# A graph network with LSTM readout on one core: VectorE's preparation reordered, weights turned during the first layer, biases added in VectorE's evictions

## What is computed

```python
def L0(x, A):                              # graph layer with two batch norms
    A_norm = A + eye
    deg = sum(A_norm, 0) + sum(A_norm, 1) - diagonal(A_norm)
    A_hat = A_norm * rsqrt(deg)[:, None] * rsqrt(deg)[None, :]
    h = relu(batchnorm(einsum('nm,bmd->bnd', A_hat, x) @ W1.T + b1))   # 128 -> 256
    return batchnorm(h @ W2.T + b2)                                    # 256 -> 128

def L1(x, adj):
    h = relu(einsum('ts,bsh->bth', adj, x @ Wg0 + bg0))
    h = relu(einsum('ts,bsh->bth', adj, h @ Wg1 + bg1))
    for p in 1, 2, 3, 4:                   # LSTM over windows of p nodes
        last = lstm_last(Wih[p-1], Whh[p-1], bih[p-1], bhh[p-1], windows(h, p))
        h[:, p-1::p] = last
    return h

x = layernorm(x + L0(x, adj))
out = layernorm(x + L1(x, adj))
```

## Time and profile before

| what | value |
|---|---|
| time, median of 3 runs | 824.11 us (822.83 to 824.62) |
| the profiled execution: its own time, its span | 823.75 us, 821.8 us |
| TensorE busy, matmuls | 767.1 us (93%) |
| VectorE, ScalarE, GpSimd busy | 645.2, 565.2, 316.0 us |
| chain that ended last, by engine | PE 56%, DVE 11%, ACT 7% |
| first aggregate starts | 16.75 us |
| stage 2's first product starts | 117.19 us |
| second group's first product starts (group 1) | 202.89 us |
| stage 4's first product starts | 399.47 us |
| one group of stage 3, from the 3rd to the 14th | 13.31 us |

### The profile page before, as it was taken

How to read it: one execution, slowest core, us unless ns; L and a number is a source line. 1 busy time by engine, 2 the same in 40 slices (tenths; PEclk the granted TensorE clock), 3 DMA queues, 4 the chain that set the end, 5 groups by cost and what they waited for, 6 DMA issues and landing times.

```text
span 821.8 us, 11917 instructions
## 1 busy us (share of the span) xinstructions
PE 767.1 (93%) x3920; PEld 427.4 (52%) x3920; DVE 645.2 (79%) x1363; ACT 565.2 (69%) x892; POOL 316.0 (38%) x282
## 2 busy tenths in 40 slices
PE   3999969978999999999999999999999999999993
PEld 2666633336676767667544444444444444555441
DVE  5455557767677777775598878799999999998998
ACT  0777748854777777767788867777666757656662
POOL 0000000006886767764000000009087947376692
PEclk9999969997999999999999999999999999999997
DMA  6333130001313132320070000000100112102012
GB/s 173 102 100 102 51 102 0 0 0 50 104 53 104 51 104 65 91 76 28 0 307 1 1 1 0 1 1 1 39 26 15 39 39 84 67 18 65 1 39 90
DMA packets 63126, 45.06 MB, mean 55 GB/s; under 512 B 1593, under 2 KB 61538, under 8 KB 62050
## 3 DMA queue, kind: packets, MB, share of 16 engines
q1 hardware_dynamic: 63074, 44.40, 17.7%
HBM read 27.61 MB, written 16.78 MB: 54 GB/s over the span
## 4 chain that ended last, share of the span: by engine, by line
PE 56%; DVE 11%; ACT 7%; issue 1%; POOL 1%; DVEq 0%
PE ps L612 10%; PE ps L613 10%; PE ps L621 9%; PE ps L617 6%; PE ps L626 6%; PE ps L618 6%; ACT work L813 4%; PE ps L688 3%; DVE work L1002 3%; ACT work L820 2%; DVE store L1012 2%; DVE store L1007 2%; DVE work L988 1%; DVE store L1056 1%; PE ps L666 1%
## 5 line engine op out<-in xcount | busy, mean ns | idle before, releaser
L813 ACT ACTIVATE work<-ps,gate_bias 128x512 f32<-128x512 f32 (+1 forms) x449 | 279.7, 681 | 63.6 <-PE ps L626 45.7
L612 PE MATMUL ps<-store,wih 128*128 128x512 f16 (+1 forms) x449 | 168.9, 376 | 2.7 <-issue 1.5
L613 PE MATMUL ps<-store,wih 128*128 128x512 f16 (+1 forms) x449 | 168.9, 376 | 0.0
L621 PE MATMUL ps<-store,wih 128*128 128x512 f16 (+1 forms) x449 | 158.0, 376 | 0.0
L510 POOL TENSOR_TENSOR end_mv<-end_mv,minus_half 128x12 f32<-128x12 f32 (+1 forms) x16 | 30.8, 1926 | 266.1 <-DVE end_mv L1031 266.1
L1002 DVE TENSOR_TENSOR work<-work 128x512 f32<-128x512 f32 (+1 forms) x129 | 89.6, 695 | 36.9 <-ACT work L820 36.9
L501 POOL TENSOR_SCALAR ring<-ring,ln_mv 128x128 f32<-128x128 f32 x120 | 117.4, 991 | 2.7 <-POOL ln_mv L491 2.5
L820 ACT ACTIVATE work<-store 128x512 f32<-128x512 f32 (+1 forms) x97 | 60.5, 623 | 66.7 <-DVE store L995 51.9
L617 PE MATMUL ps<-store,whh 128*128 128x512 f16 (+1 forms) x248 | 93.1, 376 | 0.0
L618 PE MATMUL ps<-store,whh 128*128 128x512 f16 (+1 forms) x248 | 93.1, 376 | 0.0
L626 PE MATMUL ps<-store,whh 128*128 128x512 f16 (+1 forms) x248 | 93.0, 376 | 0.1
(11 more groups left out here) (124 smaller groups left out, 1229.3 us busy)
## 6 DMA issues: line engine op xcount, KB each, us to landing
ring<-in_x_dram SPq DMA_DIRECT2D x32, 256.0 KB, 2.9
ring<-in_x_dram SPq DMA_DIRECT2D x16, 512.0 KB, 5.2
x_scratch<-ring SPq DMA_DIRECT2D x16, 512.0 KB, 3.5
ring<-x_scratch SPq DMA_DIRECT2D x5, 1024.0 KB, 4.9
out_dram<-ring SPq DMA_DIRECT2D x5, 768.0 KB, 3.6
store<-x_scratch SPq DMA_DIRECT2D x3, 1024.0 KB, 14.1
out_dram<-store SPq DMA_DIRECT2D x3, 768.0 KB, 3.5
out_dram<-ring SPq DMA_DIRECT2D x5, 256.0 KB, 2.3
```

The lines of the kernel that those rows point to most:

```text
L612: nc.tensor.matmul(acc(j), w_hi, x_hi, start=True, stop=False)
L613: nc.tensor.matmul(acc(j), w_lo, x_hi, start=False, stop=False)
L621: last = nc.tensor.matmul(acc(j), weights(wih, j)[0], x_lo, start=False, stop=u.first)
L813: nc.scalar.activation(acts[:, n % 2, gate, 0:u.cols], ps[:, gate_bank(q), 0:u.cols], ACT.Tanh if gate == G else ACT.Sigmoid, bias=gate_bi ...
```

## The change

1. VectorE's preparation is put in another order. It starts when adj is loaded, without waiting for TensorE's transpose; `ahatT` becomes the 11th step, then w1T, `vec`, w2T, the row sums, four copies of `minus_c` = -(row sum x bg0) and the gate biases. Four steps (`u1_bias` = bg1 - minus_c by Wg1) come after chunk 8 of stage 1. The f16 splits are gone. Steps that nothing near needs no longer wait for themselves (`step` beside `link`). TensorE and ScalarE wait for the step they need instead of for the last.
2. TensorE turns the weights inside stage 1, one job behind the chunks 12, 14, ... 24, and so do ScalarE's and VectorE's parts of it. One 128-column product (for `u1_bias`) is added behind chunk 8. Stage 1's loops, and SyncE's loop of loads, are written out instead of being loops of the machine.
3. A small Sigmoid at ScalarE's start (`act_warm`) loads its function table; no other load of a table stands in ScalarE's list after it (before: one at the first copy, one at the first gate).
4. In stage 3 the bias products (L686, L706) are left out. With C = row sum x bg0, relu(z + C) = max(z, -C) + C: VectorE takes the maximum of the bank and `minus_c` (`relu_h0`), and adds `u1_bias` in the eviction of u1 (`bias_u1`), which brings in C by Wg1 and bg1. Both evictions move from ScalarE to VectorE. `hidden_hi` moves from VectorE to ScalarE for the units in the groups; in stage 4 it stays on VectorE. VectorE's and ScalarE's order within a group is new.
5. bg0 is loaded as one more small vector, ahead of the gate biases, and no longer broadcast.

The diff's core:

```diff
+            def turn_weights(job):
+                pe.wait_ge(ld_lstm, 32)
+                if job == 0:
+                    pe.wait_ge(prep_dve, PREP_STEPS)
                 wait(pe, w_lo_done, job - 1)
                 for j in range(4):
                     last = nc.tensor.transpose(ps[:, 6 + job % 2, j * P:(j + 1) * P],
                                                lstm_rows[:, job * 4 + j, :], ident[:])
                 last.then_inc(w_turned, 1)
 
+            pe.wait_ge(prep_dve, AHAT_STEP)
+            aggregate(0)
+            pe.wait_ge(ld_vec, 9 * 16)
+            nc.tensor.transpose(ps[:, 6, 0:P], vec_rows, ident[:]).then_inc(prep_pe, 1)
+            nc.tensor.matmul(ps[:, 5, 0:P], ones[:], adjT[:], start=True, stop=True).then_inc(prep_pe, 1)
+            pe.wait_ge(prep_dve, W1T_STEP)
+            for c in range(CHUNKS):
+                if c == 1:
+                    pe.wait_ge(prep_dve, RS_STEP)
+                if c + 1 < CHUNKS:
+                    aggregate(c + 1)
+                channels(c)
+                if c == U1_BIAS_AT:
+                    pe.wait_ge(prep_dve, MINUS_C_STEP)
+                    pe.wait_ge(ld_wg, 32)
+                    nc.tensor.matmul(ps[:, 6, 0:P], minus_c[:, 0, :], wg1_sb[:], start=True, stop=True)\
+                        .then_inc(prep_pe, 1)
+                if c in W_JOB_AT:
+                    turn_weights(W_JOB_AT.index(c))
 
...
-                    nc.tensor.matmul(ps[:, H0[h], :], bias_l[:, 0, :], bias_bt[:].rearrange("p b n -> p (b n)"),
-                                     start=True, stop=False)
                     nc.tensor.matmul(ps[:, H0[h], :], wg0_sb[:], z_slot(g)[:, h * CB:(h + 1) * CB, :].rearrange(
-                        "p b n -> p (b n)"), start=False, stop=True).then_inc(h0_summed, 1)
+                        "p b n -> p (b n)"), start=True, stop=True).then_inc(h0_summed, 1)
...
-                    nc.tensor.matmul(ps[:, GNN[h], :], bias_l[:, 1, :], bias_tb[:].rearrange("p n b -> p (n b)"),
-                                     start=True, stop=False)
                     by_time = ps[:, GNN[h], :].rearrange("p (n b) -> p n b", b=CB)
                     for b in range(CB):
                         last = nc.tensor.matmul(by_time[:, :, b], u1[:, h * CB + b, :], adjT[:],
-                                                start=False, stop=(b == CB - 1))
+                                                start=True, stop=True)
...
-            act.wait_ge(prep_dve, PREP_STEPS)
-
-            def copy_agg(c, q):
+            act.wait_ge(consts_done, 6)
+            nc.scalar.activation(act_warm[:], ones[:, 0:1], ACT.Sigmoid)
...
+            def hidden_hi(n):
+                u = UNITS[n]
+                act.wait_ge(hid_done, n + 1)
+                nc.scalar.activation(unit_output(u, 0), columns(acts[:, n % 2, O, :], u), ACT.Copy).then_inc(hi_done, 1)
...
-                relu_h0(g, 0)
-                relu_h0(g, 1)
                 for n in FILLS[g][:1]:
                     gates(n)
-                copy_u1(g, 0)
+                    tanh_cell(n)
+                for n in FILLS[g][1:]:
+                    gates(n, (0, 1))
                 for n in FILLS[g][:1]:
-                    tanh_cell(n)
-                copy_u1(g, 1)
+                    hidden_hi(n)
                 for n in FILLS[g][1:]:
-                    gates(n)
+                    gates(n, (2,))
                     tanh_cell(n)
                 gnn_hi(g, 0)
                 gnn_hi(g, 1)
+                for n in FILLS[g][1:]:
+                    hidden_hi(n)
...
+            rsum, csum, diag, deg, dinv = (small[:, k:k + 1] for k in range(5))
             dve.wait_ge(consts_done, N_CONSTS)
+            dve.wait_ge(ld_adj, 16)
+            link(nc.vector.tensor_tensor(a_norm[:], adj_n[:], ident[:], ALU.add))
+            step(nc.vector.reduce_sum(rsum, a_norm[:], AX_X))
+            link(nc.vector.tensor_tensor(tmp_pp[:], a_norm[:], ident[:], ALU.mult))
+            step(nc.vector.reduce_sum(diag, tmp_pp[:], AX_X))
             dve.wait_ge(prep_pe, 1)
             link(nc.vector.tensor_copy(adjT[:], ps[:, 0, 0:P]))
...
             dve.wait_ge(dinv_done, 1)
             link(nc.vector.tensor_scalar(tmp_pp[:], a_norm[:], dinv, None, ALU.mult))
             assert steps[0] == SCALED_STEP
-            dve.wait_ge(prep_pe, 2)
+            dve.wait_ge(prep_pe, 3)
+            step(nc.vector.tensor_scalar(ahatT[:], ps[:, 4, 0:P], dinv, None, ALU.mult))
+            assert steps[0] == AHAT_STEP
...
-            link(nc.vector.tensor_tensor(split16[:, 1, :], ps[:, 2, 0:P], split16[:, 0, :], ALU.subtract))
-            link(nc.vector.tensor_scalar(split16[:, 1, :], split16[:, 1, :], ident[:, 1:2], None, ALU.mult))
+                step(nc.vector.tensor_copy(w1T[:, h, :], ps[:, 7, h * P:(h + 1) * P]))
+            assert steps[0] == W1T_STEP
+            dve.wait_ge(prep_pe, 4)
+            step(nc.vector.tensor_copy(vec[:], ps[:, 6, 0:P]))
+            assert steps[0] == VEC_STEP
+            for h in range(H1):
+                step(nc.vector.tensor_copy(w2T[:, h, :], ps[:, 7, (2 + h) * P:(3 + h) * P]))
+            dve.wait_ge(prep_pe, 5)
+            link(nc.vector.tensor_copy(row_sums[:], ps[:, 5, 0:P]))
+            assert steps[0] == RS_STEP
...
+                step(nc.vector.tensor_scalar(minus_c[:, b, :], row_sums[:], vec[:, VBG0:VBG0 + 1], -1.0,
+                                             ALU.mult, ALU.mult))
+            assert steps[0] == MINUS_C_STEP
+            step(nc.vector.tensor_tensor(gate_bias[:], vec[:, VIH:VIH + NG], vec[:, VHH:VHH + NG], ALU.add))
+
+            def u1_biases():
+                dve.wait_ge(ld_bg, 16)
+                dve.wait_ge(prep_pe, 6)
+                for b in range(CB):
+                    step(nc.vector.tensor_tensor(u1_bias[:, b, :], bg1_rows, ps[:, 6, 0:P], ALU.subtract))
+                assert steps[0] == PREP_STEPS
...
+            for c in range(CHUNKS):
+                channel_stats(c)
+                if c == U1_BIAS_AT:
+                    u1_biases()
+                if c in W_JOB_AT:
+                    weights_lo(W_JOB_AT.index(c))
 
             def batch_norm(first, n, rstd_count, gamma, beta, step0):
 
...
+            def relu_h0(g, h):
+                dve.wait_ge(h0_summed, 2 * g + h + 1)
+                nc.vector.tensor_tensor(h0T[:, h * CB:(h + 1) * CB, :].rearrange("p b n -> p (b n)"), ps[:, H0[h], :],
+                                        minus_c[:].rearrange("p b n -> p (b n)"), ALU.max).then_inc(h0_copied, 1)
+
+            def bias_u1(g, h):
+                dve.wait_ge(u1_summed, 2 * g + h + 1)
+                nc.vector.tensor_tensor(u1[:, h * CB:(h + 1) * CB, :].rearrange("p b n -> p (b n)"), ps[:, U1[h], :],
+                                        u1_bias[:].rearrange("p b n -> p (b n)"), ALU.add).then_inc(u1_copied, 1)
+
             def gnn_lo(g):
                 for h in range(2):
                     dve.wait_ge(gnn_hi_done, 2 * g + h + 1)
...
                     residual(g + 2, 1)
+                relu_h0(g, 0)
+                relu_h0(g, 1)
+                if g + 2 < GROUPS:
                     x1_moments(g + 3)
-                for n in FILLS[g]:
+                bias_u1(g, 0)
+                for n in FILLS[g][:1]:
                     cell(n)
+                bias_u1(g, 1)
+                for n in FILLS[g][:1]:
                     hidden(n)
-                    hidden_hi(n)
+                for n in FILLS[g][1:]:
+                    cell(n)
+                for n in FILLS[g][:1]:
                     hidden_lo(n)
+                for n in FILLS[g][1:]:
+                    hidden(n)
                 gnn_lo(g)
+                for n in FILLS[g][1:]:
```

160 lines of the change are left out of this document (53 added, 107 removed).

## The result

The changed kernel takes **796.8 us** (median of 4 runs, 795.62 to 797.14) beside 824.13 (822.83 to 824.62) for the kernel before: ratio 0.967, 95% interval 0.965 to 0.969. Predicted were 799.9, in a range of 793.5 to 807.0. The profiled execution took 796.76 us, its span is 794.7, 27.1 less than before.

The account below looks back on a forecast made before the run. TensorE, busy 93% of the span, was taken as the bound, so gains come from its gaps or queue. Terms -9.0 + 3.3 - 7.3 - 11.2 = -24.2 took the span from 821.8 to 797.6, time 799.9; range 793.5 to 807.0.

Parts of the forecast that it names:

- start, to the third aggregate: Before stage 1's steady part: `ahatT` made at 6.95, first aggregate at 7.4 instead of 16.75, 6.15 us onward kept; 9.35 earlier.
- chunk 4 late: Start: chunk 4 of x, queued behind Whh, lands at about 19.1 while TensorE wants it at 18.75; 0.35 charged.
- weights in stage 1: Stage 1: seven transpose jobs at 0.44 plus a 128-column product at 0.22, all on TensorE's path; +3.3.
- gap between the stages 1 and 2: Relu starts when scale and shift are ready, at 108.30 instead of 115.64, no longer behind ScalarE's weight copies; -7.3.
- clock in stage 2: Second layer's first products: TensorE still idles about 6.8 us beforehand, its clock falls as before; no change.
- group 0: Stage 3's first group: saves nothing, waits for GpSimd's scaling; moments ahead of `bias_u1` are not covered by LSTM units; +0.5.
- stage 4: Last stage: same code, same order, no change; 422.3 us from its first product to the end.
- The table load: Stage 3, group 1: the 1.28 us load between two gates delays B and the next `turn_z`, and goes; -1.3.
- The ring: Groups of stage 3: VectorE and ScalarE steps set a period of 12.5 instead of 13.31; -10.5 over 13 groups.
- a period of 12.0 with no gap at `turn_z`: Stage 3 groups: sign that the predicted mechanism is wrong and there is no ring; 12.5 with a gap was expected.
- TensorE's queue sets the period: Rival, stage 3: high part and evictions cheap or overlapping better, groups last 12.0, 6.5 less, time 793.4; chance 0.13.
- GpSimd rival: Stage 3: GpSimd becomes the bound beside fuller VectorE; slower kernel, 827 at 1.6 per scaling instead of 1.00; chance 0.02.

## Why the prediction was right, and where it was not

The total came out 3.1 us too high. That it came so close is in part luck: going by the table, the groups 1 to 13 gave 6.05 us more than forecast, and all other rows together 3.15 less. By its own steps, predicted and measured:

| step | predicted | measured |
|---|---|---|
| start, to the third aggregate | -9.35 | -8.69 |
| chunk 4 late | +0.35 | 0 |
| weights in stage 1 | +3.3 | +3.29 |
| gap between the stages 1 and 2 | -7.3 | -7.45 |
| clock in stage 2 | 0 | +0.58 |
| group 0 | +0.5 | +1.54 |
| groups 1 to 13, period and table load | -10.5 - 1.3 | -17.85 |
| groups 14, 15 | +0.1 | +0.44 |
| stage 4 | 0 | +1.04 |
| sum | -24.2 | -27.1 |

The measured column is the difference of neighbouring rows of the table at the head of this part. Thirteen periods of 13.31 - 11.93 are 17.94, which is all of the 17.85. The table load does not show in it because two things of one size cancel there: the groups 1 and 2 lasted 0.75 longer than two steady ones before the change, and 0.83 longer in the changed kernel (24.69), where half rate lies in group 1.

**The start** held: nine steps and the power, a first aggregate at 7.15 for 7.4. But the part from the first to the third aggregate took 7.06, not 6.15. The small products took 0.70 (9.19 to 9.89), the wait of 0.32 for ScalarE's first copy went, and the first channels took 2.62 instead of 2.05, as they ran at half rate for longer. The first two were in the prediction's text as 0.6 and 0.3, but it kept 6.15 and so put their difference at nothing. No run takes the new order of the preparation back by itself; that the earlier `ahatT` brings the start forward is read from the two traces. **Chunk 4** was mechanically right and not due: TensorE came 0.7 later than I had it, and the chunk was there. In seven traces in which TensorE came to it earlier it was waited for, by 0.18 to 1.31, and its aggregate then started between 18.81 and 19.57, around the foretold 19.1.

**The weights** held in every number: stage 1 grew by 3.29, and the gap shrank by 7.45; putting them back cost 4.6.

**The ring** was the right mechanism and its size was off. I had walked it at 12.5; the chain walks the same steps at 11.94: VectorE up to the hop 6.03 for 6.44, ScalarE 3.50 for 3.55, VectorE's end 2.41 for 2.53. The term that failed is "two residuals 1.31, two maxima 1.31, `bias_u1` 0.65". I had taken the distance from the first residual to the moments in the earlier trace rows, and it holds a wait: the moments need the second residual's result. In the new order the maxima follow, which do not need it: from the first residual to the first maximum are 1.20 (243.75 to 244.95), and as much from there to the moments. The moments take 2.31 for 2.42, `bias_u1` 0.60 for 0.65. At 13 groups 0.57 makes 7.4 us. For the same reason VectorE works 10.84 per group and not 11.5. This is also why the gap at `turn_z` did not show: I had expected 0.5, and 0.10 was left of it, under the 0.16 that a product's way to its end covers in such rows. With six products fewer it shows (0.94), at the place and with the releaser that were foretold. By the prediction's own sign, a period of 12.0 with no gap at `turn_z`, there was no ring; the sign misled, since it left out that the queue and the ring can come to nearly the same length. The rival "TensorE's queue sets the period" had its time (12.0) nearly right and its mechanism not: 1.29 us less on TensorE changed nothing. But the reserve is small, for only 0.10 of 0.86 us more on TensorE was free. The two limits stand next to each other.

**The table load** was the term for which I had a row and read it wrongly. 1.28 between two gates was counted as a delay of the next group because ScalarE is in the ring. But in group 1 TensorE's queue still sets the pace (11.83 in the kernel without the early Sigmoid, the queue's own length), and the ring takes over only later. The groups 1 and 2 before the change lasted 12.79 + 14.58 = 27.37, 0.75 over two steady ones; from 202.89 to group 3's first product, in the trace of the kernel before:

```profile
230.26 1.95 PE L676 MATMUL ps<-adjT,ring 128*128 128x128 f32 x16
```

So at most 0.75 of the 1.3 was there to be gained, and no run took the load out of the kernel before to show that it was the load's. In the changed kernel putting the load back cost 0.02. The Trainium skill, "ScalarE: Activation LUTs", section "What ACT_TABLE_LOAD costs", adds a drain of about 1380 ns to the 1283 of the load. No run here shows it: the load took 1283 ns, the next activation began 0.02 later, and both loads together did not move the median.

**Group 0** had its direction right: the moments on VectorE ahead of `bias_u1` hold TensorE, 1.89 us. Group 0 costs 1.5 instead of 0.5, since the idle stretch brings the clock down; the half rate is worth 1.25 of it. **Stage 4** got 1.0 longer with the same code for the same reason: TensorE waits 2.33 ahead of it instead of 1.46. That "stage 4: same code, no change" and "the clock still falls as before: no change" leave out the clock is the second failed step: in the changed kernel's trace it cost 0.6 in stage 2, 1.25 in group 0, 0.8 in the groups 1 and 2, and 1.0 in stage 4.

## What to carry to other kernels

When you walk a ring of steps that will follow each other without a wait, take each step's cost from rows where the same engine runs two of them back to back, not from a distance that holds a wait or a shown duration; here some 0.05 us on each of ten steps made 7.4 us. After summing, put the queue of the engine that was the bound beside the ring: if they come within 1%, as 11.83 and 11.93 here, further work on either alone buys next to nothing. And price every idle stretch of TensorE twice, once for itself and once for the half rate that can follow it; filling the stretches with products that nobody reads gave 6.1 us here, with everything else unchanged.

## What was not expected of the hardware

- After idle stretches of 5.3 and 6.7 us TensorE ran at 1.2 GHz in every trace read here, unless they were filled. After stretches of 1.7 to 2.3 us it did in some executions and not in others of much the same kernel: ahead of gnn's products in group 0 the clock fell after 1.89 us in the changed kernel and stayed up after 1.89 in the one with four products more and after 1.72 in the one without the early Sigmoid; ahead of stage 4, after 2.33, it fell in five traces and stayed up in two. The six executions of one kernel (without the early Sigmoid) lie at 792.8 to 793.0 or at 796.8 to 797.3, and nothing between. What decides it was not tried.
- In the gap between the stages 1 and 2 turning weights (8 + 8 + 8 + 4 transposes between waits of 0.6 and 4.9 us) did not keep the clock up; a fill without pause (29 products, 6.42 us) did.
- A table load on ScalarE between two gates cost the kernel nothing measurable, at the start and in group 1.
- GpSimd's scaling of a row took 0.78 us in group 0 (6.25 for eight), where VectorE was idle for a part of the time, and 1.0 to 1.04 in the steady groups beside a VectorE that works 10.84 of 11.93. The mean of its 120 scalings rose from 991 to 1019 ns with the change: it got slower and not faster, as the prediction's GpSimd rival feared, but by 28 ns where that rival needed 330. Beside which of VectorE's steps it slows was not tried.
